# TensorE's general path as one loop, and a kernel end in halves of the batch with the totals added on GpSimd

## The reference

```python
VOCABS = [12500, 6250, 2500, 1250, 625, 250, 1000, 500, 200, 100]   # EMB_DIM 64, BATCH 1024
embs = [jnp.dot(x, w) for x, w in zip(xs, ws)]
emb_sum = embs[0]
q_emb = jnp.dot(xs[0] ** 2, ws[0] ** 2)
for i in range(1, len(xs)):
    emb_sum = emb_sum + embs[i]
    q_emb = q_emb + jnp.dot(xs[i] ** 2, ws[i] ** 2)
fm_ans = 0.5 * (emb_sum ** 2 - q_emb)
return jnp.concatenate([fm_ans] + embs, axis=-1)
```

## Time and profile before

| | us |
|---|---|
| median of 3 runs | 287.22 |
| lowest, highest | 287.17, 287.44 |
| profiled execution | 289.03 |
| its span, first to last instruction | 287.3 |
| time of it outside the span | 1.7 |
| VectorE busy | 240.2 (84%) |
| ScalarE busy | 227.6 (79%) |
| TensorE busy | 218.8 (76%) |
| GpSimd busy | 88.3 (31%) |
| moved by DMA | 113.90 MB, 396 GB/s over the span |

### The profile page before, as it was taken

How to read it: one execution, slowest core, us unless ns; L and a number is a source line. 1 busy time by engine, 2 the same in 40 slices (tenths; PEclk the granted TensorE clock), 3 DMA queues, 4 the chain that set the end, 5 groups by cost and what they waited for, 6 DMA issues and landing times.

```text
span 287.3 us, 2928 instructions
## 1 busy us (share of the span) xinstructions
PE 218.8 (76%) x878; PEld 154.5 (54%) x878; DVE 240.2 (84%) x236; ACT 227.6 (79%) x271; POOL 88.3 (31%) x68
## 2 busy tenths in 40 slices
PE   0459989999887888877887887887787888777760
PEld 0338757666555555555554554555555555555550
DVE  3742999999999998888889888988888898888960
ACT  0769999998987888788977877877877888787940
POOL 0442527326214304109224224314314304104000
PEclk9999999999999999999999999999999999999995
DMA  7999999999999999999999999999999999999932
GB/s 235 403 406 413 408 416 415 420 412 420 416 423 414 420 420 417 419 413 417 422 419 417 419 420 421 419 422 418 416 419 421 419 419 412 416 411 425 404 134 80
DMA packets 22419, 113.90 MB, mean 396 GB/s; under 512 B 3728, under 2 KB 4752, under 8 KB 10752
## 3 DMA queue, kind: packets, MB, share of 16 engines
q1 hardware_dynamic: 16976, 106.90, 90.5%
q10 hardware_dynamic: 5424, 6.79, 6.6%
HBM read 110.79 MB, written 2.88 MB: 396 GB/s over the span
## 4 chain that ended last, share of the span: by engine, by line
DMA 62%; issue 23%; DVE 6%; ACT 3%; PE 2%; POOL 1%; ACTq 1%; DVEq 0%; POOLq 0%
DMA x_ring<-in_x_dram 57%; DVE is_one L450 5%; DMA whole<-in_w_dram 5%; ACT is_set L287 2%; PE sums L376 1%; ACT turned L298 1%; POOL low L357 1%; PE sums L383 1%; DVE total L487 0%; ACT whole L280 0%; ACTq L267 0%; POOL high L355 0%; DVE results L490 0%; DVE results L493 0%; ACTq L274 0%
## 5 line engine op out<-in xcount | busy, mean ns | idle before, releaser
L450 DVE TENSOR_SCALAR_CACHE_REDUCE is_one<-x_ring 128x2048 uint8<-128x2048 f32 (+2 forms) x108 | 226.2, 2116 | 28.5 <-DMA x_ring<-in_x_dram 28.4
L287 ACT ACTIVATE is_set<-x_ring 128x2048 fp32r<-128x2048 uint32 (+2 forms) x108 | 192.1, 1783 | 37.1 <-DMA x_ring<-in_x_dram 37.0
L376 PE MATMUL sums<-is_set,low 128*128 128x512 f32 x398 | 135.3, 422 | 59.0 <-ACT is_set L287 52.2
L376 PE MATMUL sums<-is_set,high 128*128 128x512 f32 x398 | 126.2, 399 | 0.0
L376 PEld LDWEIGHTS sums<-is_set,low 128*128 128x128 f32 x398 | 68.7, 191 | 103.4 <-ACT is_set L287 53.8
L376 PEld LDWEIGHTS sums<-is_set,high 128*128 128x128 f32 x398 | 76.2, 191 | 17.8
L355 POOL CAST high<-whole 128x1024 fp32r<-128x1024 f32 (+5 forms) x31 | 27.0, 872 | 170.2 <-ACT whole L280 170.2
L357 POOL TENSOR_TENSOR low<-whole,high 128x1024 fp32r<-128x1024 f32 (+5 forms) x31 | 60.7, 1957 | 2.5
L287 ACT ACTIVATION_READ_ACCUMULATOR is_set<-x_ring 128x1 f32 (+1 forms) x108 | 20.6, 191 | 0.0
L280 ACT ACTIVATE whole<-whole 128x512 f32<-128x512 f32 (+5 forms) x31 | 16.7, 540 | 4.0 <-DMA whole<-in_w_dram 4.0
L383 PE MATMUL sums<-identity,turned 128*128 128x128 f32 x80 | 10.8, 280 | 0.8 <-ACT turned L328 0.8
(11 more groups left out here) (17 smaller groups left out, 3.7 us busy)
## 6 DMA issues: line engine op xcount, KB each, us to landing
x_ring<-in_x_dram SPq DMA_DIRECT2D x91, 1024.0 KB, 18.4
x_ring<-in_x_dram SPq DMA_DIRECT2D x16, 512.0 KB, 10.2
whole<-in_w_dram ACTq DMA_DIRECT2D x19, 256.0 KB, 7.4
out_dram<-results SPq DMA_DIRECT2D x10, 256.0 KB, 12.5
x_ring<-in_x_dram SPq DMA_DIRECT2D x1, 448.0 KB, 6.2
whole<-in_w_dram ACTq DMA_DIRECT2D x2, 192.0 KB, 5.6
whole<-in_w_dram ACTq DMA_DIRECT2D x2, 160.0 KB, 7.1
out_dram<-results ACTq DMA_DIRECT2D x1, 256.0 KB, 2.1
```

Of the source, the lines that this page charges most:

```text
L287: nc.scalar.activation(is_set[chunk.k % SETS][0:chunk.rows, 0:chunk.n * BATCH], x_of(chunk).bitcast(U32), ACT.Sign, accum_out=set_counts[0 ...
L376: last = nc.tensor.matmul(sums[:, summing(n, half), :], w, x[0:chunk.rows, at:at + HALF], start=first, stop=False, skip_group_check=True)
L450: nc.vector.tensor_scalar(is_one[chunk.k % 2][0:chunk.rows, 0:chunk.n * BATCH], x_of(chunk), 1.0, None, ALU.is_equal, ALU.add, accum_out=o ...
```

## The change

1. The general path of TensorE is one loop over all 199 tiles, with one body of 16 matmuls; short last tiles are handled by SyncE and VectorE (rows that the tile doesn't have are repeated from the tile ahead and get zero weights).
2. `total` keeps the layout in which the sums come, 128 rows by 1024. GpSimd adds the copied sums of each table to it, at the end of a later group of weights; VectorE adds nothing within the loop. After the ninth table GpSimd multiplies it by `weight` (1 for the embedding rows, 0.5 for the squares).
3. `turn` moves the 64 embedding rows alone, into one PSUM bank. The steps after a table stand 1, 2 and 3 chunks behind it instead of 2, 3 and 5.
4. The last chunk goes by halves of the batch on ScalarE and TensorE. For each half VectorE adds the last table's sums from PSUM to `total`, TensorE turns the total, ScalarE squares it, VectorE finishes the term, and SyncE stores it. The last embedding is copied in one piece, behind that.
5. The odd counts grow by one column; VectorE has one small copy more in the check, and two small memsets at the start.

```diff
-COPY_AFTER, TURN_AFTER, ADD_AFTER = 2, 3, 5
+COPY_AFTER, TURN_AFTER, TAKE_AFTER = 1, 2, 3
...
 def copy_sums(n):
     act.wait_ge(x_multiplied, END[n])
     if n >= 2:
         act.wait_ge(sums_turned, n - 1)
+        act.wait_ge(added, n - 1)
...
             n = NT - 1
-            act.wait_ge(x_multiplied, END[n])
             act.wait_ge(sums_turned, n - 1)
-            for half in range(2):
+            for half, blocks in enumerate(halves):
+                act.wait_ge(added, n + half + 1)
                 nc.scalar.activation(turned[n % 2][:, half * HALF:(half + 1) * HALF],
                                      sums[:, summing(n, half), :], ACT.Copy).then_inc(sums_copied, 1)
-            for half, blocks in enumerate(halves):
-                act.wait_ge(added, n + half + 1)
-                nc.scalar.activation(results[:, LAST + 1, blocks, :], turning(n)[:, blocks, 0, :],
-                                     ACT.Copy).then_inc(emb_copied, 1)
-            act.wait_ge(emb_copied, NT + 1)
+                act.wait_ge(total_turned, half + 1)
+                nc.scalar.activation(half_squared[:, blocks, :], turned_total[:, blocks, 0, :], ACT.Square,
+                                     scale=0.5).then_inc(squared_sum, 1)
+            act.wait_ge(sums_turned, NT)
+            nc.scalar.activation(results[:, LAST + 1, :, :], turning(n), ACT.Copy).then_inc(emb_copied, 1)
+            act.wait_ge(emb_copied, NT)
             act.dma_start(out[LAST + 1], results[:, LAST + 1, :, :]).then_inc(stored, 16)
...
@@ gpsimd, behind the split of a group
+                for n in adds_after.get(g, []):
+                    pool.wait_ge(sums_copied, n + 1)
+                    if n:
+                        pool.wait_ge(added, n)
+                        nc.gpsimd.tensor_tensor(total[:, :], total[:, :], turned[n % 2][:, :], ALU.add
+                                                ).then_inc(added, 1)
+                    else:
+                        nc.gpsimd.tensor_copy(total[:, :], turned[n % 2][:, :]).then_inc(added, 1)
+            weigh()
...
@@ tensor, general path
-                for t in range(NT):
-                    base = sum(TILES[:t])
-                    def multiply_tile(i, rows):
...
-                    if TILES[t] > 1:
-                        with pe.Fori(0, TILES[t] - 1) as i:
-                            multiply_tile(i, P)
-                    multiply_tile(TILES[t] - 1, TAIL[t])
+                with pe.Fori(0, sum(TILES)) as i:
...
@@ vector, end
+            dve.wait_ge(total_weighted, 1)
+            for half in range(2):
+                dve.wait_ge(half_multiplied, half + 1)
+                at = slice(half * HALF, (half + 1) * HALF)
+                nc.vector.scalar_tensor_tensor(out=total[:, at], in0=sums[:, summing(n, half), :],
+                                               scalar=weight[:, 0:1], in1=total[:, at], op0=ALU.mult,
+                                               op1=ALU.add).then_inc(added, 1)
...
+                dve.wait_ge(squared_sum, half + 1)
+                nc.vector.scalar_tensor_tensor(out=results[:, 0, blocks, :], in0=half_squared[:, blocks, :],
+                                               scalar=2.0, in1=turned_total[:, blocks, 1, :],
+                                               op0=ALU.mult, op1=ALU.subtract).then_inc(fm_ready, 1)
```

More of the change, by code:

```diff
@@ L100 @@
 NGROUPS, NCHUNKS = len(GROUPS), len(CHUNKS)
+G_ORDER = [9] + [t for t in range(NT) if t != 9]
 BEGIN = [min(g.chunks[0].k for g in GROUPS if g.place == n) for n in range(NT)]
@@ L237, in _ @@
             with sp.If(odd != 0):
[L238 to L251 removed]
+                base = zeros = 0
@@ L286, in count_set @@
                     act.wait_ge(x_multiplied, chunk.k - SETS + 1)
[L287 to L290, removed]
+                parts = 2 if chunk.k == NCHUNKS - 1 else 1
+                length = chunk.n * BATCH // parts
+                for part in range(parts):
+                    at = slice(part * length, (part + 1) * length)
+                    nc.scalar.activation(
+                        is_set[chunk.k % SETS][0:chunk.rows, at], x_of(chunk).bitcast(U32)[:, at],
+                        ACT.Sign, accum_out=set_counts[0:chunk.rows, chunk.k + part:chunk.k + part + 1]
+                        ).then_inc(set_counted, 1)
             def copy_sums(n):
@@ L347, in _, with weigh @@
             nc.gpsimd.tensor_copy(probe_high[:, :], probe[:, :]).then_inc(probe_ready, 1)
+            def weigh():
+                pool.wait_ge(added, NT - 1)
+                nc.gpsimd.tensor_scalar(total[:, :], total[:, :], weight[:, 0:1], None, ALU.mult
+                                        ).then_inc(total_weighted, 1)
+            adds_after = {}
+            for n in range(NT - 1):
+                ready = min(END[n] - 1 + COPY_AFTER, NCHUNKS - 1)
+                at = min(CHUNKS[ready].group.g + AHEAD - 1, NGROUPS - 1)
+                adds_after[at] = adds_after.get(at, []) + [n]
             for group in GROUPS:
@@ L379, in multiply, with multiply_last @@
                 last.then_inc(x_multiplied, 1)
+            def multiply_last(chunk):
+                group, n = chunk.group, chunk.group.place
+                for half in range(2):
+                    pe.wait_ge(set_counted, chunk.k + half + 1)
+                    for part in (low, high):
+                        last = nc.tensor.matmul(
+                            sums[:, summing(n, half), :], part[group.pair][0:chunk.rows, chunk.at, :],
+                            is_set[chunk.k % SETS][0:chunk.rows, half * HALF:(half + 1) * HALF],
+                            start=False, stop=False, skip_group_check=True)
+                    last.then_inc(half_multiplied, 1)
             def turn(n, blocks):
                 for b in range(blocks.start, blocks.stop):
-                    last = nc.tensor.transpose(turning(n)[:, b, :, :],
-                                               turned[n % 2][:, b * P:(b + 1) * P], identity[:, :])
-                last.then_inc(sums_turned, 1)
-            pe.wait_ge(constants, 4)
+                    last = nc.tensor.transpose(turning(n)[:, b, :], turned[n % 2][0:D, b * P:(b + 1) * P],
+                                               identity[0:D, 0:D])
+                return last
+            pe.wait_ge(constants, 6)
             pe.wait_ge(unit_ready, 1)
@@ L397, in _ @@
                             pe.wait_ge(emb_copied, n - 1)
-                            pe.wait_ge(added, n - 1)
-                        turn(n, slice(0, NB))
+                        turn(n, slice(0, NB)).then_inc(sums_turned, 1)
             n = NT - 1
+            for half, blocks in enumerate(halves):
+                pe.wait_ge(added, n + half + 1)
+                for b in range(blocks.start, blocks.stop):
+                    last = nc.tensor.transpose(turned_total[:, b, :, :], total[:, b * P:(b + 1) * P],
+                                               identity[:, :])
+                last.then_inc(total_turned, 1)
             pe.wait_ge(emb_copied, n - 1)
-            pe.wait_ge(added, n - 1)
             for half, blocks in enumerate(halves):
                 pe.wait_ge(sums_copied, n + half + 1)
-                turn(n, blocks)
+                last = turn(n, blocks)
+            last.then_inc(sums_turned, 1)
             pe.wait_ge(odd_ready, 1)
@@ L465, in _ @@
             for chunk in CHUNKS:
                 count_ones(chunk)
-                for n in due(chunk.k, ADD_AFTER):
-                    add(n)
+            n = NT - 1
+            dve.wait_ge(total_weighted, 1)
+            for half in range(2):
+                dve.wait_ge(half_multiplied, half + 1)
[3 more added lines that the diff above has]
+                                               op1=ALU.add).then_inc(added, 1)
```

145 lines of the change are left out of this document (78 added, 67 removed).

## The result

The changed kernel takes 285.68 us (median of 4 runs, 285.19 to 287.05) against 287.33 for the kernel before (4 runs): a ratio of 0.994, interval 0.9914 to 0.9966. It is faster, by 0.6% and not by the forecast 1.7%, and its time lies above the stated range. The profiled execution took 287.05, with a span of 285.2; the other three had spans of 283.5 to 284.2.

The account below looks back on a forecast made before the run. The DMA stream of x was taken to set the pace, followed by the work chain and TensorE's branch. Savings of 3.6 us (branch) and 1.4 (stores), 0 in the middle, took 287.22 to 282.2; range 281.2 to 284.6.

Parts of the forecast that it names:

- Part 1, the mechanism: TensorE's branch over the general path: jumping some 64 instructions instead of 1216 cuts it from 5.18 to 0.05-0.07 us.
- Part 1, the size: End of the kernel: of 5.1 us off TensorE's own end only 3.6 show, since SyncE is late next.
- Part 4: Last table and term by halves: the last store lands and SyncE branches at 281.5 instead of 282.9, 1.4 us earlier.
- flag: Value loaded for the branch at the end: SyncE at its wait by 280.9, ahead of the last landing at 281.5.
- The wait ahead of that copy: ScalarE waits for the ninth table's transposes ahead of chunk 106: later starts slip 0.5 us, costing 0.15 on the path.
- GpSimd's weighing: Last table's total multiplied on GpSimd: 1.04 us, at worst 2.39, done by 272.1 with cover of 3.5 us.
- Parts 2 and 3: Middle of the kernel: GpSimd's additions and smaller, earlier transposes stay hidden under the stream, cost 0 (bounds 0 and 0.8).
- the reserve: Small tables: chunk 16's load goes out 2.1 to 2.8 us ahead of the landing before it, just feeding the queue.
- the ring: Slots for x: early embedding copies delay loads at small tables, yet the queue stays fed; cost 0 (bounds 0 and 0.8).
- Rival B: Slots for x run dry in the small tables, each starved microsecond costing one; 1 to 2 us give 283.2 to 284.2; 10%.
- Rival A: End of the kernel: the branch still costs TensorE its 5.18 us, time 286.7 us; 7%.
- rival C: Small tables: slow GpSimd additions delay splits, so starvation takes 5 us and more; 288.7 with 6.5 lost; 3%.

Follow-up runs that it names:

- runs with added bodies: Changed kernel with 2, 5 or 11 more unrolled bodies of 16 f32 matmuls in TensorE's skipped general path, single runs: 286.71, 287.12 and 289.18 us.
- second profile: Kernel before, run once more with only a comment edited, for another profile: 287.42 against 287.44 us, ratio 1.0003.
- the loop alone: Kernel before with only the general path's single TensorE loop and what it needs on SyncE and VectorE: 285.69 us, ratio 0.9931.
- the old places: Changed kernel with the first eight tables' three steps back at 2, 3 and 5 chunks behind: 283.67 us, then 283.39.
- the run with 24 matmuls put in: Changed kernel with 24 constant matmuls on TensorE ahead of the first chunk and 8 ahead of the third table: 284.5 us, ratio 0.9913.

## Why the prediction was wrong

- **Part 1, the mechanism: right.** The branch fell to 226 ns, SyncE is late next, and the runs with added bodies show distance as the cause: a jump over 384 instructions took 0.47 us and one over 768 took 4.05. That the time is a fetch is still an inference. The Trainium skill (Runtime: NRT & Kernel Launch, "Instruction fetch mechanics") says that a taken branch out of the current window of two pages, of 256 instructions each, forces a fetch, and gives TensorE's instruction memory 2048 instructions. The runs agree with a window of 512 and not with one of 2048.
- **Part 1, the size: wrong.** The step was "It lies 1.8 above the median of the runs, which I take as the same for both". The 1.8 us were no constant: they lay in and around the branch that the change removes, so the 3.6 us that stood behind SyncE in that profile hold them. In the second profile 2.0 stood there, and the loop alone measured 1.8. This is worth 1.8 us of the miss.
- **Part 4: right in its shape, 0.6 short.** Last landing ScalarE's, halves out ahead of it, flag not in the way. From chunk 105's landing to SyncE's branch I forecast 12.1 us (281.5 less 269.40); it is 11.5. Most of the difference is there at the copy of the ninth embedding: forecast 2.8 us behind chunk 105 (272.2 less 269.4), measured 2.3. My sum let it start 0.3 behind the end of the transposes, where its own rows have 0.04; after has 0.03. The wait ahead of that copy was 0.32, under my 0.5. In the table the end is 2.1 to 2.3 shorter than with the loop alone, forecast 1.4. GpSimd's weighing took longer than my upper bound of 2.39 and still hid: 2.86 us from 273.18, done 2.8 us ahead of VectorE's use at 278.85 (after, timeline):

```profile
273.18 2.86 POOL L376 TENSOR_SCALAR total<-total,weight 128x1024 f32<-128x1024 f32 x1
```

- **Parts 2 and 3: the step that failed most.** "I put this at 0 (bounds 0 and 0.8)." ScalarE's places came out near my upper ends: chunk 8 at 32.71 (32.6), the load of chunk 16 at 34.8 (34.6). What failed is the reserve read from it. I placed the landing ahead of it at 36.7, from chunk 16's landing before less its own bytes. In the kernel before chunk 15 in fact landed at 36.3 (issued at 29.2, 7.1 to land), and in after, with no other load of x in the queue behind it, it came at 35.5, which left 0.7 us and not 2.1. And I took a lone transfer's 2.0 us as what a fed queue needs, where chunk 17, out 1.8 us ahead of the landing before it, still ran in a stretch at 246 GB/s. The runs put the term at 2.0 to 2.3 us: that much the old places win back (285.68 to 283.67 and 283.39). In the profiled run the loss is 3.1 (273.02 less 269.90).
- **The sum.** With the sizes measured: 287.3, less 1.8 for the loop, less 2.0 for the end (285.69 to 283.67), plus 2.0 for the ring, is 285.5; measured 285.68. That it closes proves little, since each size is a difference between two of these runs. The profiles say the same by another way: against the loop alone the end is 2.1 us shorter and chunk 105 3.1 later, in a run that was 1.4 above its median. Rival B named the mechanism and had 10% and 1 to 2 us. Its evidence, four microseconds of lag and one more wait with each small table, was in the prediction and deserved more. Rival A fell with the branch of 226 ns, rival C with the run that keeps GpSimd's additions and loses nothing.
- **Open.** Why the same far branch takes 3.6 in one run and 5.2 in another (the traces hold a lead, untested: with 5.2 two packets of the instruction queue move during the branch and none in the 10 us ahead of it, and in the three profiles with 3.6 to 4.1 one moves during it and one 3 to 8 us ahead); whether the time is the fetch; how the ring's loss divides between the three early places; why the loss at the ring spreads over the runs of after (spans 283.5 to 285.2); and whether the early places would still cost if TensorE ran at full pace there, since in every profile with them alone it was slow until 28 to 31 us.

## What to carry to other kernels

Read the sequencers' branches by line, since no busy share shows them; and before a duration from one profile goes into a sum, compare that profile's span with the usual runs and ask which row holds the difference. A step that waits for a slower engine may be put early only where the buffers behind it have slack: with small tables the ring has least, so the same step can stand early at the last table and late at the first ones, as in the fastest kernel here. Look for a starved queue in the bytes moved, since the busy share can stay at nine tenths while they fall by a quarter. Cut each run at the last data's arrival, and two effects that cancel in the total stand apart.

## What the runs showed of the hardware

- A far taken branch on TensorE is an abrupt cost, with the step between 384 and 768 instructions here, and its size varies by 1.6 us between profiles (3571 to 5182 ns).
- TensorE ran the small tables' matmuls 0.43 us apart until 29 us in after, with a granted clock of 0.50 (1.2 GHz); before, the same spacing from 19.4 to 24 us stood beside a granted clock of 1.00 in the record. In the run with 24 matmuls put in it stood idle for 3.13 us ahead of 19.58 and was slow again from there. The run with 5 bodies has a granted clock of 1.00 throughout and still the slow spacing until 30 us. The pace of the matmuls in the timeline says more than the clock's record.
- VectorE's wait for x is no measure of starvation: between 17 and 60 us before has 0.4 us of it, the kernel with the old places 8.4 and after 10.5, and only after lost time in the stream.
